# First cross attention of a Perceiver block: the ring, the lags and the entries of one software pipeline, each a step further back

## The reference

```python
    def _L0_xattn_ref(x, y, Wq, bq, Wk, bk, Wv, bv, Wkv_dca, bkv_dca, qn_w, qn_b, kn_w, kn_b, kn_dca_w, kn_dca_b, Wo, bo):
        ...
        q = _ln((x @ Wq + bq).reshape(b, s1, H, HD), qn_w, qn_b)
        kv = jnp.concatenate([y_main @ Wk + bk, y_main @ Wv + bv], axis=-1)
        kv = kv.reshape(b, s2, H, 2 * HD)
        k = _ln(kv[..., :HD], kn_w, kn_b)
        v = kv[..., HD:]
        qT = q.transpose(0, 2, 1, 3)
        ctx = _attn(qT, k.transpose(0, 2, 1, 3), v.transpose(0, 2, 1, 3))
        ...
        ctx = ctx + DCA_WEIGHT * ctx_dca
        return ctx @ Wo + bo
```

## Time and profile before

| | |
|---|---|
| median of 3 runs | 2568.33 us (2560.31 to 2572.9) |
| the profiled execution's own time | 2568.98 us |
| its span | 2567.2 us |
| stage x0b, steps and drain | about 142 to 820 us of the span |
| PE busy in the span | 2280.6 us (89%) |
| DVE, ACT, POOL busy | 1631.9, 1206.5, 1033.1 us |

### The profile page before, as it was taken

How to read it: one execution, slowest core, us unless ns; L and a number is a source line. 1 busy time by engine, 2 the same in 40 slices (tenths; PEclk the granted TensorE clock), 3 DMA queues, 4 the chain that set the end, 5 groups by cost and what they waited for, 6 DMA issues and landing times. The chain is left out here.

```text
span 2567.2 us, 45868 instructions
## 1 busy us (share of the span) xinstructions
PE 2280.6 (89%) x16206; PEld 1805.9 (70%) x16212; DVE 1631.9 (64%) x2618; ACT 1206.5 (47%) x2236; POOL 1033.1 (40%) x718
## 2 busy tenths in 40 slices
PE   4589999999997799978988999999999988888766
PEld 2577777777774688866766788888888866666644
DVE  3547877787776333335532688888888874676663
ACT  1346565665652233323203676676667653333242
POOL 3049888988884000000110355455445550110320
PEclk8699999999997899988998999999999998999879
DMA  3000000001000222103312000000000002111200
GB/s 110 1 26 27 27 2 27 27 27 46 4 2 1 80 65 65 53 14 89 77 35 94 26 25 11 20 27 19 18 18 27 1 12 85 46 37 33 79 1 17
DMA packets 104280, 89.92 MB, mean 35 GB/s; under 512 B 32752, under 2 KB 82432, under 8 KB 104080
## 3 DMA queue, kind: packets, MB, share of 16 engines
q1 hardware_dynamic: 103792, 87.28, 11.3%
q0 software_dynamic: 288, 0.00, 0.0%
HBM read 86.22 MB, written 1.05 MB: 34 GB/s over the span
## 5 line engine op out<-in xcount | busy, mean ns | idle before, releaser
L2258 POOL TENSOR_TENSOR xT<-xT,x1b_ring 128x512 f32<-128x512 f32 (+1 forms) x176 | 248.4, 1411 | 213.4 <-ACT x1b_ring L2388 206.5
L923 POOL TENSOR_TENSOR x0b_krstd<-x0b_krstd,minus_half 128x24 f32<-128x24 f32 x64 | 267.0, 4171 | 91.4 <-DVE x0b_krstd L986 85.4
L943 POOL TENSOR_TENSOR xT<-xT,x0b_ring 128x512 f32<-128x512 f32 (+1 forms) x170 | 240.4, 1414 | 38.4 <-ACT x0b_ring L1160 24.3
L111 DVE TENSOR_TENSOR x1b_plo<-x1b_ring,x1b_phi 128x512 fp32r<-128x512 f32 (+1 forms) x208 | 221.8, 1066 | 6.4 <-issue 4.6
L2403 ACT ACTIVATE x1b_ring<-x_ps,x1b_keymask 128x512 f32<-128x512 f32 (+1 forms) x208 | 143.1, 688 | 132.1 <-DVE xT L2330 126.8
L1160 ACT ACTIVATE x0b_ring<-x0b_ring 128x512 f32<-128x512 f32 (+1 forms) x208 | 131.2, 631 | 151.8 <-DVE x0b_ring L1004 143.7
L1036 DVE TENSOR_TENSOR x0b_ring<-x_ps,x0b_krstd 128x512 f32<-128x512 f32 (+1 forms) x208 | 142.8, 686 | 74.1 <-PE x_ps L828 72.0
L116 PE MATMUL x_ps<-x1b_qy,x1b_yT 128*128 128x512 f32 (+1 forms) x416 | 175.7, 422 | 4.3 <-ACT x1b_ring L2403 2.9
L116 PE MATMUL x_ps<-x1b_phi,x1b_yv 128*128 128x512 f32 (+1 forms) x416 | 166.6, 400 | 1.5 <-ACT x1b_out_sb L2370 1.5
L2330 DVE SCALAR_TENSOR_TENSOR xT<-x_ps,x1b_keymask,xT 128x512 f32<-128x512 f32 (+1 forms) x176 | 131.2, 746 | 57.6 <-PE x_ps L118 56.7
L117 PE MATMUL x_ps<-x1b_qy,x1b_yT 128*128 128x512 f32 (+1 forms) x416 | 164.5, 395 | 0.0
(11 more groups left out here) (588 smaller groups left out, 5737.9 us busy)
## 6 DMA issues: line engine op xcount, KB each, us to landing
x_y<-in_ctx_dram SPq DMA_DIRECT2D x8, 1536.0 KB
x_y<-in_ctx_dram SPq DMA_DIRECT2D x24, 512.0 KB, 3.9
a_wn<-in_L_attn_W_Q_dram SPq DMA_DIRECT2D x16, 256.0 KB, 3.0
a_wn<-in_L_attn_W_K_dram SPq DMA_DIRECT2D x16, 256.0 KB, 3.5
a_wn<-in_L_attn_W_V_dram SPq DMA_DIRECT2D x16, 256.0 KB, 4.0
a_won<-in_L_attn_W_O_dram SPq DMA_DIRECT2D x16, 256.0 KB, 2.9
x1a_wq<-in_L_xattn_Wq_dram SPq DMA_DIRECT2D x4, 1024.0 KB, 10.5
x1c_wo<-in_L_xattn_Wo_dram SPq DMA_DIRECT2D x8, 512.0 KB, 7.3
```

The source lines that it names most:

```text
L111: return v.tensor_tensor(lo, exact, hi.bitcast(F32), ALU.subtract)
L923: ins = g_.tensor_tensor(r, r, c.minus_half[:, 0:8].unsqueeze(1).broadcast_to([P, whole, 8]), ALU.pow)
L943: g_.tensor_tensor(total[half][0:m, :], old, src, ALU.add).then_inc(summed, 1)
L2258: g_.tensor_tensor(total[half][0:m, :], old, src, ALU.add).then_inc(summed, 1)
```

## The change

The ring of tiles has 19 places instead of 18, the shift (and exponential, and sum) is 16 steps behind the scores instead of 15, the product with the values 18 instead of 17. The row chains are all a step later, and the walk of the last sequence is one step longer. The tables of entries are new.

```diff
-        SLOTS, LAG_SUB, LAG_PV = 18, 15, 17
+        SLOTS, LAG_SUB, LAG_PV = 19, 16, 18
...
-        HERE = entries("0:T02 0:K030 1:K031 2:W03 3:T03 3:K100 4:K101 5:W10 5:V0 6:T10 6:K110 6:V1 7:K111 7:V2 8:W11 8:V3 "
-                       "9:T11 9:K120 9:V4 10:K121 11:W12 11:V5 12:T12 12:V6 13:K130 14:K131 14:V7 15:W13 15:V8 16:T13 "
-                       "18:V9 20:Va 21:Vb 23:Vc")
-        AHEAD = entries("12:Y00 13:Y01 15:Y10 16:K000 16:Y11 17:K001 18:W00 19:T00 19:K010 20:K011 21:W01 22:T01 22:Y20 "
-                        "22:Y21 23:K020 24:K021 24:Y30 24:Y31 25:W02")
+        HERE = entries("0:T02 0:K030 1:K031 2:W03 2:K100 3:T03 3:K101 4:W10 5:T10 5:K110 6:K111 7:W11 7:V0 8:T11 8:K120 8:V1 "
+                       "9:K121 9:V2 10:W12 10:V3 11:T12 11:V4 12:V5 13:K130 13:V6 14:K131 15:W13 15:V7 16:T13 17:V8 19:V9 "
+                       "20:Va 21:Vb 22:Vc")
+        AHEAD = entries("11:Y00 12:Y01 16:Y10 16:Y11 17:K000 18:K001 19:W00 20:T00 20:K010 21:K011 22:W01 23:T01 23:Y20 "
+                        "23:Y21 24:K020 24:Y30 25:K021 25:Y31 25:W02")
...
-            for n in range(TILES + 19 if part == "last" else TILES):
-
-                for what, at in (("sums", 30), ("inverse", 31), ("maxima", 13)):
+            for n in range(TILES + 20 if part == "last" else TILES):
+
+                for what, at in (("sums", 31), ("inverse", 32), ("maxima", 14)):
...
-                    f = half_at(part, n, 15)
+                    f = half_at(part, n, 16)
...
-                    f = half_at(part, n, 30)
+                    f = half_at(part, n, 31)
...
-                    f = half_at(part, n, 31)
+                    f = half_at(part, n, 32)
...
-                    f = half_at(part, n, 13)
+                    f = half_at(part, n, 14)
```

## The result

| | before | after |
|---|---|---|
| median | 2572.76 us (2560.31 to 2586.89, 10 runs) | 2593.71 us (2587.56 to 2600.44, 10 runs) |
| ratio after / before | | 1.0076, 95% interval 1.0052 to 1.0101 |
| the profiled execution | 2568.98 us | 2600.44 us |

The changed kernel is slower, by some 21 us. Forecast were 2578 us and a range up to 2588. The sign of the sum was right, its size was not.

The account below looks back on a forecast made before the run. TensorE's work plus its waits were taken to bound the kernel. Crossings +11.9, other entries -1.0, first sequence +1.0, last -1.7 and clock -0.3 gave +9.9 us, so 2578 us was forecast, range 2557 to 2588.

Parts of the forecast that it names:

- The sign of the sum: Whole program: all terms together come to +9.9 us, so the changed kernel is slower, by 0.38%.
- the other entries: W03, W10, W11, W13 outside the crossing: new waits 1.7 against 2.0 removed; -0.3, taken as -0.15 us a sequence.
- the first new wait: Step 24 of the crossing: K020 waits 1.4 us for the split of Y21, which Vc covered before.
- the clock: TensorE at the crossings: the old fall goes, -1.8 us; one new fall in seven crossings, +1.5; together -0.3.
- What bounds the kernel: Stage x0b: TensorE's work plus its waits set the end; about 3.6 us of waits a sequence can be won.
- what the row chains gain: Maxima, sums, inverse a step later: L888's 1.57 us goes, also 0.94, 0.44, 0.40 and W12's 0.23.
- the pattern of step 22: T01, Y20, Y21 in step 23 keep step 22's timing: shift of next step at 4.32, splits end at 4.17.
- this adds no wait: Ring of 19, shift 16, product 18: slot reuse keeps its distances, so no wait; cost is one step more of drain.
- Second new wait: Step 25 of the crossing: W02 waits 1.85 us for both squares, through shift, exponential, copy, square.
- Crossing +1.7: Steps 23 to 0: new waits 1.4 and 1.85 less L888's 1.57 make +1.7 us a time, seven times.
- the banks that L853 and L795 waited for are free by then: Sums and inverse a step later: a V of about 1.5 us or a whole step stands between.
- The rival that it falls at every crossing: TensorE's clock drops at all seven crossings: 10.5 us in place of 1.5, 2587 us; chance 0.20, shared with a longer crossing.

Follow-up runs that it names:

- no_add: Changed kernel with GpSimd's additions of exponentials left out in steps 22 to 25 of every sequence but the last; 2580.04 us, 1.0051 of the kernel before.
- ring20: Changed kernel with a ring of 20 places instead of 19, nothing else; 2593.04 us, 1.0112 of the kernel before.
- fill_both: Changed kernel with unread identity transposes at the crossings, 12 ahead of K020's waiting matmul and 8 ahead of W02; 2581.16 us, 1.0055 of the kernel before.
- after_again: The changed kernel itself measured once more, as anchor on its own chip; 2593.13 us, 1.0097 of the kernel before.
- fill_w02: Changed kernel with 8 identity transposes ahead of W02's wait for the squares in the seven crossings; 2587.60 us, 1.0088 of the kernel before.
- w11_step8: Changed kernel with Vc and K021 in step 24, neighbours swapped in four steps, W11 in step 8 and T11 in step 9; 2558.85 us, 0.9962 of before.
- each half of the change: Kernel before with only the new ring, lags and row chains (V0 to V4 a step later), 1.0168; with only the new tables, 1.0150.
- a mended table: The table of w11_step8, on the changed kernel's ring and lags; 2558.85 us, 0.9962 of the kernel before.
- best1: Changed kernel with Vc and K021 in step 24, K110/T10, V7/W13 and K100/W03 swapped, K030 ahead of T02; 2575.51 us, 1.0027 of the kernel before.

## Why the prediction was wrong, step by step

The way the time would go and both new waits were forecast. Three terms failed: the other entries, put at -0.15 a sequence, were +0.8, because the waits for banks had been put at nothing; the first new wait, put at 1.4, was 2.16; and the clock, put at one fall in seven crossings, fell at six in one execution and at five in another.

- *What bounds the kernel; what the row chains gain.* Right: PE plus its waits set the stage, and the waits of L888, L853, L862, L795 went, in all six sequences.
- *First new wait, 1.4.* The place was right, the term too small: 2.16. I took over the pattern of step 22, in which the scores are followed 0.84 us later by the scaling and the split ends at 4.17. Now the scaling comes 298.73 - 297.53 = 1.20 after the scores, and the maximum takes 1.18 where it took 0.84 at this place in the kernel before; the split ends at 300.87 + 1.53 - 297.53 = 4.87. Both delays come from POOL: the scaling waited 0.86 for an earlier sum (the prediction's "this adds no wait" for the ring was wrong there), and an addition ran beside the maximum (298.81 to 300.08). no_add shows it: with the additions left out the scaling does not wait, the maximum takes 0.69 and K020's wait is 1.32. ring20 shows that of the two it is the addition beside the maximum that counts: without the wait for the sum the maximum took 1.53 and K020 still waited 2.16. The Trainium skill (SBUF — State Buffer, SBUF: two separate sides) says that a DVE operation with two SBUF inputs and a GpSimd operation that reads SBUF exclude each other on a shared pair of ports. The traces agree: the maximum took 1.53 us beside an addition (ring20) and 0.69 without one (no_add). I had looked at it for no term.
- *Second new wait, 1.85.* Measured 1.61: the chain shift, exponential, copy, square was right to 0.24.
- *Crossing +1.7.* Measured 2.16 + 1.61 - 1.57 = 2.2.
- *Other entries, -0.15 a sequence.* Wrong, and in sign. I had costed the W entries (W11 0.9) and not one bank. W11 took 0.29, but V0 0.91 and V9 0.30 waited for the bank of the inverse and K111 0.41 for that of T10. With W03 0.31, W10 0.23 and W13 0.31 it is 2.76 against 2.0 removed: +0.8 a sequence. The sentence "the banks that L853 and L795 waited for are free by then" was true of those two and left out who came to stand on the bank of the inverse instead.
- *Per sequence* these are 2.2 + 0.8 = 3.0; fill_both, at full clock, measured 3.14, where 1.7 - 0.15 = 1.55 was forecast. This is the largest failure among the waits. The stage of fill_both ends 837.3 - 820.3 = 17.0 us later than before. The executions do not reach the stage at the same time, though: their first transposes of the context stand at 114.52 (before), 115.27 (after), 113.42 (after_again) and 112.93 (fill_both). Counted from there, the stage of fill_both is 724.4 - 705.8 = 18.6 us longer than before without a lowered clock in the middle, against 8.4 in the sum without its fall. The difference, 10.2, is what the terms give: seven times 2.2 - 1.7 and 0.8 + 0.15.
- *Clock, one fall in seven.* Wrong. The rival that it falls at every crossing came nearly true: six of seven in the profiled run, five of seven in after_again. Counted as above, the falls cost 731.0 - 724.4 = 6.6 us in after_again (17.0 us at the lower level) and 734.5 - 724.4 = 10.2 in the other execution (27.3 us), where one fall of 1.5 had been taken and the rival had 10.5. I had taken the second wait, 1.85, as lying between 1.57 (which did nothing) and 1.91 (which did), and not the first, which I had at 1.4. It was the first that mattered: at 2.16 it was followed by four of the six falls before W02 had waited at all, and by falls in fill_w02, where W02's idle was filled but for 0.5 us at most. With it at 1.32, and W02's 1.61 unchanged, one fall was left in seven crossings (no_add). The same waits do not always bring a fall (the second crossing of after has both and none), and what decides between them stays open. The error of 0.75 in the first wait thus cost twice.
- *The sum*: 18.6 of waits and 6.6 to 10.2 of clock are 25.2 to 28.8, against +9.9. The medians differ by 21 to 24.5 us. What follows the stage in the program is not changed, yet span less end of stage is 1746.9 before, 1748.9 and 1745.4 in the two profiles of the changed kernel, 1741.7 in fill_both and 1742.2 in w11_step8. It goes with the granted clock there: worked out from windows of 4 us, TensorE was at the lower level behind the stage for 176.5 us before, 185.9 and 175.6 in the changed kernel, 164.7 in fill_both and 162.0 in w11_step8. Why identical work is granted a different clock stays open.

That each half of the change is worse alone, and that a mended table on the same lags wins, says that the lags alone were not at fault: the tables were written for where the scores stand, not for who holds a bank or a port. Whether the lags of before would do as well with a table made with the same care was not run.

## What to carry to other kernels

When entries move against row chains in a ring of banks, list for each entry who had its bank last and where that one is read, before looking at data dependencies: here 0.9 us at V0, and 4.1 us in another order, came from a bank alone. A wait that is removed was often the cover of the next one (T02's 0.82 in front of K030). The moves that paid put work whose data are old in front of a wait (Vc ahead of K020) or took an entry out of a bank's way (W11 a step behind the norm). Where TensorE waits for a microsecond or more, read the granted clock behind the wait as well, and look also at two shorter waits close together: 0.72 and 1.05 us (best1) were followed by a fall in five of seven sequences, where single ones of 1.57 had none in six.

## What the hardware did that I had not expected

- A maximum of two 128 x 512 tiles in SBUF takes 0.69 us on VectorE; beside a GpSimd addition of such tiles it took 1.18 (after) and 1.53 (ring20) at the crossing. In the trace after, all 76 that met no addition took 0.69. Leaving out four additions a sequence gave about 12 us (1.0097 to 1.0051), of which 0.84 a crossing are the shorter wait; most of the rest goes with the falls of the clock, 3.4 us at the lower level instead of 17.0.
- The granted clock falls about when TensorE resumes from an idle, in after up to 0.6 us later and in fill_w02 up to 1.7: at 216.3 behind a single idle of 2.16 us that ended at 215.93, at 393.8 behind 1.61 us of idle that followed 2.16 us some five microseconds earlier, while 1.32 and 1.61 at the same places left it up from 223 to 470 us.
- 20 transposes of nothing at each crossing made the program 12.0 us faster.
